# One-core graph, mixing and FFN kernel: byte-addressed operands, one slot for both one-hots of a pair, a table of visit numbers, bounds loaded during the FFN matmuls

## What is computed

```python
xn = _layernorm(x, axis=-1)
# graph part: keep the 32 largest of each row of xn @ W_neigh, sum them over the edges src -> dst
h_sparse = _maxk(h_neigh, MAXK)
summed = jax.ops.segment_sum(h_sparse[src], dst, num_segments=n)
neigh = summed / jnp.maximum(deg, 1.0)[:, None]
# mixing part: linear attention with a gate from a small MLP
out = jnp.einsum('bnhd,bhdv->bnhv', q, context).reshape(b, n, c)
mixed = out * gate @ Wproj + bproj
x = x + (h_self + neigh) + mixed
# FFN part: a top-half selection of the rows by a router weight, then gelu(x @ w1 + b1) @ w2 + b2
x = x + _L0_ffn_ref(_layernorm(x), ...)
```

## Time and profile before

| | |
|---|---|
| median of 3 runs | 2023.87 us |
| lowest, highest | 2014.73 us, 2028.19 us |
| the profiled execution, time | 2022.68 us |
| its span, first to last instruction | 2020.8 us |
| PE busy | 1572.2 us (78%) |
| DVE busy | 1247.4 us (62%) |
| POOL busy | 1202.6 us (60%) |
| mean granted TensorE clock | 0.863 of full |

### The profile page before, as it was taken

One profiled execution on the slowest core, in us unless ns is written; L12 is line 12 of the kernel. 1 busy time (PEld: TensorE's weight loads), 2 busy tenths in 40 slices (PEclk: granted clock), 3 DMA queues, 4 the chain that ended last, 5 costly groups with the idle time before them and its releaser, 6 DMA issues. The chain is left out here.

```text
span 2020.8 us, 40760 instructions
## 1 busy us (share of the span) xinstructions
PE 1572.2 (78%) x8607; PEld 1137.6 (56%) x8608; DVE 1247.4 (62%) x3826; ACT 438.7 (22%) x974; POOL 1202.6 (60%) x1348
## 2 busy tenths in 40 slices
PE   1798454778878778888978988887888888888771
PEld 0354253355556556666656656666666666667561
DVE  5899973877656423677634566643666535666256
ACT  0354231011111111222212222222222222222120
POOL 2254544767777777677777576773767653655200
PEclk8799776998888787999889888998889988889885
DMA  9122114333334565343477333484334572334664
GB/s 203 38 82 69 58 45 127 102 96 107 109 110 119 145 163 153 93 117 111 119 181 180 89 106 105 119 200 114 107 88 114 146 177 70 101 88 112 146 144 127
DMA packets 150932, 236.40 MB, mean 117 GB/s; under 512 B 26368, under 2 KB 115420, under 8 KB 150780
## 3 DMA queue, kind: packets, MB, share of 16 engines
q0 software_dynamic: 52480, 142.82, 25.5%
q10 hardware_dynamic: 70374, 65.55, 12.9%
q1 hardware_dynamic: 27926, 26.20, 5.4%
HBM read 208.46 MB, written 26.01 MB: 116 GB/s over the span
## 5 line engine op out<-in xcount | busy, mean ns | idle before, releaser
L640 POOL DMA_INDIRECT ring<-rows_d,stage x1088 | 1079.4, 992 | 505.0 <-issue 294.8
L1003 PE MATMUL bank<-ring,region_v 128*125 x1260 | 427.5, 458 | 71.2 <-SPq L540 45.3
L1371 DVE SCALAR_TENSOR_TENSOR region_v<-iota,tile_start,dstT 128x500 f16 x315 | 234.0, 743 | 192.2 <-issue 149.2
L1003 PEld LDWEIGHTS bank<-ring,region_v 128*125 x1260 | 192.8, 153 | 209.9 <-issue 137.3
L975 PE MATMUL bank<-region_k 128*125 x622 | 223.6, 454 | 86.9 <-issue 70.5
L954 PE MATMUL bank<-region_v 128*125 128x256 f32 x848 | 233.8, 437 | 31.1 <-issue 31.1
L1402 DVE TENSOR_SCALAR region_k<-iota,win_start,region_k 128x500 f16 x622 | 233.1, 416 | 0.0
L1396 DVE SCALAR_TENSOR_TENSOR region_k<-iota,region_k 128x250 f16 x311 | 131.7, 424 | 150.2 <-issue 121.7
L1004 PE MATMUL bank<-ones,region_v 128*125 128x2 f16 x1260 | 220.4, 175 | 0.0
L954 PEld LDWEIGHTS bank<-region_v 128*125 128x125 f32 x848 | 182.4, 221 | 64.7 <-issue 32.5
L947 PEld LDWEIGHTS bank<-region_v 128*128 128x128 f32 x1664 | 196.7, 194 | 2.8
(11 more groups left out here) (287 smaller groups left out, 1912.4 us busy)
## 6 DMA issues: line engine op xcount, KB each, us to landing
region_k<-rows_d ACTq DMA_DIRECT2D x30, 672.0 KB
ring<-rows_d,stage POOLq DMA_INDIRECT x1088
region_k<-rows_d ACTq DMA_DIRECT2D x10, 784.0 KB
region_v<-xT_d ACTq DMA_DIRECT2D x53, 125.0 KB, 5.2
xT_d<-region_r ACTq DMA_DIRECT2D x51, 125.0 KB, 2.2
rows_d<-region_r SPq DMA_DIRECT2D x50, 125.0 KB
region_k<-in_x_dram ACTq DMA_DIRECT2D x50, 125.0 KB
yw_d<-region_v ACTq DMA_DIRECT2D x50, 125.0 KB
```

The costliest lines, as they stand in the source:

```text
L640: pool.indirect_dma_start(out=ring[:, c, :], out_offset=None, in_=rows_d, in_offset=bass.IndirectOffsetOnAxis(ap=stage[:, c:c + 1], axis=0 ...
L1003: m = pe.matmul(total, onehot_s, row_s, start=False, stop=False, skip_group_check=True)
L1371: dve.scalar_tensor_tensor(out=hot_slots[:, bass.ds(hot, GC), :], in0=iota[:, 0:T].rearrange("p (a t) -> p a t", a=1).to_broadcast([128, G ...
```

## The change

Four things are changed.

1. **Byte addresses.** The operands of groups and pairs are cut from views of bytes, so that the register holds a byte offset, and no register operation scales an index to an address.
2. **One slot for a pair.** The low one-hots and the key one-hots of a pair lie in one slot of 2504 bytes instead of in two buffers, so that one register value reaches them all.
3. **Visit numbers in the table.** The table of window bounds holds the running number of the pair's visit (pair number plus window number plus 1) instead of the pair number. The loop over pairs runs over that, and the waits take it as it is. Group visits are counted from one in the same manner.
4. **Loads elsewhere.** The loads of a position's bounds move. On TensorE `look_ahead` goes from the end of the position to between `ffn_down` and `ffn_up`, and the window bounds are loaded behind `ffn_up` (class `Windows`). On VectorE the window bounds of the next position are loaded after the FFN rows, in front of `hot_ahead`, and at the head of the first position of an iteration.

```diff
+        SLOT_HOT, SLOT_RING, SLOT_PAIR = GC * T * 2, GC * 2 * C * 2, PAIR * (LW + KEYS) * 2
+        KEYS_AT = PAIR * LW * 2
+
+        def part(octets, slots, slot, at, first, length):
+
+            return octets[:, first:first + (slots - 1) * slot + length][:, bass.ds(at, length)]
...
+        class Windows:
+            def look(self, i, windows):
+                for k in windows:
+                    at = i * NW + (k + T_WIN)
+                    first = load(self.engine, at, 1, NPAIR + NEDGE) if k == 0 else self.end
+                    self.end = load(self.engine, at + 1, 2, NPAIR + NEDGE)
+                    cuts = [first, self.engine.snap((first + self.end) // 2), self.end] if k == 0 else [first, self.end]
+                    self.spans[k] = cuts
...
-                def count(c):
-                    visited = pe.snap(c + w)
-                    pe.wait_ge(s_hot, visited + 1)
-                    slot = pe.snap(visited % HOT_PAIRS)
-                    lo, key = pe.snap(slot * (PAIR * LW)), pe.snap(slot * (PAIR * KEYS))
+                def count(v):
+                    pe.wait_ge(s_hot, v)
+                    slot = pe.snap((v % HOT_PAIRS) * SLOT_PAIR)
                     for u in range(PAIR):
-                        m = pe.matmul(out, lo_words[:, u * LW:(u + PAIR * (HOT_PAIRS - 1)) * LW + T][:, bass.ds(lo, T)],
-                                      key_words[:, u * KEYS:(u + PAIR * (HOT_PAIRS - 1) + 1) * KEYS][:, bass.ds(key, KEYS)],
-                                      start=False, stop=False, skip_group_check=True)
+                        lo = part(pair_bytes, HOT_PAIRS, SLOT_PAIR, slot, u * LW * 2, T * 2).bitcast(F16)
+                        key = part(pair_bytes, HOT_PAIRS, SLOT_PAIR, slot, KEYS_AT + u * KEYS * 2, KEYS * 2).bitcast(F16)
+                        m = pe.matmul(out, lo, key, start=False, stop=False, skip_group_check=True)
...
                 ffn_down(one, y_sum)
+                ends.look_ahead(n, s == PER - 1)
                 ffn_up(one)
+                spans.look(i, windows)
                 pe.wait_ge(s_deg, here)
...
-                ends.look_ahead(n, s == PER - 1)
 
             positions(pe, position)
...
-            dve.tensor_scalar(bounds[:, T_WIN:T_WIN + NEDGE], row_w, misc[:, 0:1], None, ALU.mult)
+            dve.scalar_tensor_tensor(out=bounds[:, T_WIN:T_WIN + NEDGE], in0=row_w, scalar=misc[:, 0:1], in1=win_first,
+                                     op0=ALU.mult, op1=ALU.add)
...
-                at = dve.snap(((g + first_group) % NG) * GC + GC)
+                at = dve.snap(((g + first_group) % NG) * (GC * 4))
                 visited = dve.snap(g + t)
-                hot = dve.snap((visited % HOT) * GC)
-                dve.wait_ge(s_oh_free, visited + 1)
+                dve.wait_ge(s_oh_free, visited)
+                hot = dve.snap((visited % HOT) * SLOT_HOT)
...
                 ends.look_ahead(n, s == PER - 1)
+                if s + 1 < PER:
+                    spans.look(i, after_windows)
                 if s != PER - 2:
                     hot_ahead(n, i, s)
...
-                if s + 1 < PER and SHARE[s + 1] == 0:
+                if s + 1 < PER:
                     hold(dve, *st.at(a))
```

More of the change, by code:

```diff
@@ L8 @@
 I32 = mybir.dt.int32
+U8 = mybir.dt.uint8
 ALU = mybir.AluOpType
@@ L245, in build @@
         row_w = region_r.take([1, NEDGE])
+        win_first = region_r.take([1, NEDGE])
+        lead = region_r.take([1, NT])
         edge_row = region_r.take([1, ND + 1, NW])
@@ L383, in build @@
         SMALL = 8 * 16
-        SETUP = 22
+        SETUP = 23
         DIGIT = 3
@@ L423, in enter @@
                 g0, self.end = self.end, self.ahead
-                return g0, self.end, self.visits + s, self.lead
+                return g0, self.end, self.visits + (s + 1), self.lead
             def look_ahead(self, n, last):
@@ L978, in count @@
+                        m = pe.matmul(out, lo, key, start=False, stop=False, skip_group_check=True)
                     m.then_inc(s_hot_free, 1)
-                if part != 1:
-                    pe.wait_ge(s_evac, w + max(k + 1, 2) - k)
+                if half != 1:
+                    pe.wait_ge(s_evac, i * NW + max(k + 1, 2))
                     pe.matmul(out[:, 0:2], zeros16[:, 0:T], zeros16[:, 0:2], start=True, stop=False, skip_group_check=True)
[L983 to L986, removed]
+                if half == 0:
+                    with pe.If(cuts[1] > cuts[0]):
+                        with pe.Fori(cuts[0], cuts[1]) as v:
+                            count(v)
@@ L987, in count_window @@
                     return
-                with pe.Fori(middle if part == 1 else pairs0, pairs1 + 1) as c:
-                    count(c)
+                with pe.Fori(cuts[-2], cuts[-1]) as v:
+                    count(v)
                 pe.matmul(out[:, 0:2], zeros16[:, 0:T], zeros16[:, 0:2], start=False, stop=True, skip_group_check=True)\
@@ L1424, in _ @@
                 with dve.Fori(0, led) as g:
-                    visit(0, g, tile_at(0, 0))
+                    visit(1, g, tile_at(0, 0) * 4)
             def hot_ahead(n, i, s):
                 if s == PER - 1:
-                    first, finals = load(dve, n + (T_G0 + 1)), load(dve, n + (T_VIS + 1))
+                    first, finals = load(dve, n + (T_G0 + 1)), load(dve, n + (T_VIS + 1)) + 1
                     led = load(dve, n + (T_LEAD + 1))
                 else:
-                    first, finals, led = ends.end, ends.visits + (s + 1), ends.lead
+                    first, finals, led = ends.end, ends.visits + (s + 2), ends.lead
+                after = dve.snap(tile_after(i, s, 1) * 4)
                 with dve.If(led > first):
                     with dve.Fori(first, led) as g:
-                        visit(finals, g, tile_after(i, s, 1))
+                        visit(finals, g, after)
             def position(n, i, s, windows):
                 g0, g1, finals, led = ends.enter(n, s)
+                if s == 0:
+                    spans.look(i, windows)
+                after_windows = range(windows.stop, windows.stop + SHARE[(s + 1) % PER])
                 tile = tile_at(i, s)
```

105 lines of the change are left out of this document (50 added, 55 removed).

## The result

The changed kernel takes 1939.9 us (median of 4 runs, 1935.5 to 1944.4) against 2023.8 us: ratio 0.959, 95% interval 0.955 to 0.963, so 84 us faster. Its span is 1938.2 us, at a mean clock of 0.874.

The account below looks back on a forecast made before the run. GpSimd's gathers were taken to bound iterations 1 and 2, TensorE iterations 3 to 5; 31 us there, 7 at the first position and 7 of clock made 45 us, so 1977 us, range 1944 to 2000.

Parts of the forecast that it names:

- Clock: Positions with windows: fuller pair stretches spare some falls to 1.2 GHz, 7 us gained, between 0 and 27.
- the clock stays up: Rival: at most positions the clock no longer falls, TensorE gains until VectorE is the bound; 1940 to 1960 us, chance 0.20.
- Window loads: TensorE, second windows in iterations 3 to 5: 0.77 of 1.10 us idle goes, 18 times, 13.9 us.
- Pairs: TensorE, iterations 3 to 5: less register work saves 0.13 us in each of 129 pairs, 16.8 us, between 0 and 38.
- rival that register instructions are no cheaper: Instructions left are packed fuller and a pair keeps its 0.93 us: 15 us gained, 1998 to 2015 us, chance 0.13.
- Groups: TensorE, iterations 3 to 5: only the first group behind a window gains, 0.1 us some 25 times, 2.5 us.
- VectorE must keep up: Iterations 3 to 5: VectorE's pairs and groups gain 45 us, more than TensorE's 31, so TensorE stays the bound.
- Cover of the moved loads: TensorE's loads behind FFN matmuls are hidden by 1.8 to 1.9 us of lead; cost 1.5 us, at first positions.
- rival that loads stop the array: The sequencer does not run ahead through `ffn_down` and `ffn_up`, each load is bare: 32 us slower, 2055 us, chance 0.04.
- First position: 46 pairs, one window load and 0.3 us, with the ring full, bring the gathers forward: 7 us gained.
- no gain in iterations 1 and 2: GpSimd's gathers set the pace there, so what TensorE or VectorE gain becomes waiting for landings: no gain counted.
- the 2 us taken off for iteration 3: GpSimd is still busy much of that iteration and would be met by some positions, so 33.2 us became 31.

Follow-up runs that it names:

- a1: The kernel before with only the window loads and the look-ahead of bounds moved to where the changed kernel has them, addresses as before: 1979.7 us.
- b2: The changed kernel with two unused loads put on TensorE at the head of each odd window: 1961.2 us.
- a5: The kernel before with byte addresses and numbering from one for groups only, on TensorE and VectorE: 1993.5 us.
- c1: The changed kernel with VectorE's four loads of a position placed around the last group's one-hot, under unfinished work: 1940.8 us.
- b4: The changed kernel with two of the four gathers of each group left out: 1762.7 us.
- b1: The kernel before with one more matmul by zero weights in each pair on TensorE: 2007.2 us.

## Why the prediction was off

The direction, the places and most mechanisms were right; the clock term was mis-sized.

- **Clock: 7 us forecast, between 0 and 27; 49 by the half-clock count.** This is the step that failed. I had seen that the fall comes right behind the thin pair stretch and priced it at some 3 us a time and 54 in all, but took an eighth of that, held that pairs would still be too thin, and capped it by VectorE's slack. The cap was too low as well: VectorE itself gained 0.22 us a pair and 0.23 a group, 63 us by my sum for it and not 45. At the 12 window positions of iterations 4 and 5 behind their first ones (31 to 36, 41 to 46) the half-clock time went from 68 us to none. The rival "the clock stays up" (1940 to 1960 us, up to 80 us gained with pairs at more than 0.13) is what happened, with 84 us just beyond its end: pairs came to 0.79 here and to a median of 0.74.
- **Window loads: 13.9 us.** The stop went as forecast (1.10 to 0.15 us). The term holds for the stop itself (19 us of rest in a1, with the look-ahead), but a1 shows 23 us of clock behind it. I had tied the clock to pairs alone; a1 and b2 show that it goes with stops too.
- **Pairs: 16.8 us, 0.13 each.** The median period went from 0.96 to 0.74 us in these iterations, 0.22 less, within my 0 to 0.30; 129 times the 0.09 more are 12 us. It is the shorter register work and not the clock: in the kernel before a pair took 0.96 us at full clock and 0.97 at half (a group 1.10 and 2.14). The rival that register instructions are no cheaper falls.
- **Groups: 2.5 us.** a5 measured 29 us for them, 18 of rest and 12 of clock in iterations 3 to 5. I had counted the first group behind a window alone. That the array is full in a run of groups is so, but the sequencer gets further ahead there, and ahead of pair matmuls TensorE was idle 10 us less in a5.
- **"VectorE must keep up": held, but its sign was wrong.** I wrote that TensorE stays the bound, and c1 bears that out: an earlier VectorE gained nothing. I also wrote that a vanishing wait of VectorE for the graph sum would mean that it has become the bound. Of the 21 positions with windows it waited at 18 in the kernel before and at two in the changed one, and that meant only that VectorE had no time to spare. Its pair came to 0.98 us, as forecast; its group gained 0.23 us, not 0.11 to 0.15.
- **Cover of the moved loads: right.** 0.1 us of idle time behind `ffn_up`. The rival that loads stop the array falls.
- **First position: 7 us forecast, 7.4 measured, and lost at once.** Iteration 1 was 6.1 us longer: GpSimd sets the pace there, and the stretch took in 7 gathers more (314 against 307): they were not brought forward with TensorE, as I had argued. b4 shows that no gain in iterations 1 and 2 was read rightly; the 2 us taken off for iteration 3 should have been 18.

By terms, of the span: rest 38 us against 31 forecast, clock 49 (an upper price, as b1 shows) against 7, and outside iterations 3 to 5 a loss of 5 instead of a gain of 7: 83 against 45.

## What to carry to other kernels

Price a stop or a thin loop on TensorE twice: by its own length, and by up to half of the half-clock time that follows it in the trace; here the second was the larger, and a filler matmul in the thin loop showed it in one run. An engine that has stopped waiting, or comes late to its last step, is not by that the bound: make it alone faster (c1) and measure at the other engine's end, and look whether the other ever meets its wait unfulfilled. And where transfers set the pace of some stages, halve them once in both kernels: it shows how much of a change's gain (here 84 of 190 us) they let through.

## What the runs showed of the hardware

- More matmuls, less time: 129 matmuls by zero weights made the kernel before 16 us faster, with the mean clock of iterations 3 to 5 at 0.95 instead of 0.89.
- In the kernel before, the clock fell to 0.50 behind a stretch without any gap over 1.1 us, only thinly filled (1.78 of 3.80 us busy); filled to 2.50 of 3.90 us (b1), the same stretch had the full clock behind it.
- In the kernel before a pair took 0.96 us at full clock and 0.97 at half, as its sequencer set the pace; a group of chunks took 1.10 and 2.14 us.
- TensorE's sequencer ran ahead of the array, but at its 315 waits for groups by no more than 15 matmuls and 15 weight loads, in both kernels.
- A semaphore increment on a sequencer that nobody waits for is not free: three a pair made VectorE's pair 0.32 us longer (0.98 to 1.30), some 0.1 us each.
- A load of a value on TensorE's sequencer took 0.30 us at a window's head, but 0.38 and 0.60 us behind `ffn_up` of the changed kernel:

```profile
L414 PEldq TENSOR_LOAD <-bounds x2: 376/486/597, 1439.8 to 1440.8; - x2
```
